# Layer 0's scores as one fp32r product of 128 rows, with its row term brought in by key quarters

## The reference

```python
B, H, W, C = 8, 32, 32, 96; NH, HD = 6, 16
# layer 0: group norm, attention with relative positions over 32x32 = 1024 tokens
attn  = einsum('bqd,bkd->bqk', q * HD**-0.5, k)
rel_h = einsum('bhwc,hkc->bhwk', r_q, Rh)          # by key row
rel_w = einsum('bhwc,wkc->bhwk', r_q, Rw)          # by key column
attn  = attn + rel_h[..., :, None] + rel_w[..., None, :]
x = x + (softmax(attn) @ v) @ proj_w + proj_b
# layer 1: layer norm, causal attention of 6 heads over the same 1024 tokens, then
# layer norm and 4 experts (96 -> 384 -> 96, GELU) of which the best 2 are mixed by a gate
```

## Time and profile before

| | |
|---|---|
| median of 3 runs | 2086.81 us (2080.82 to 2087.43) |
| profiled execution | 2086.0 us, span 2084.2 us |
| TensorE busy | 1821.2 us (87%), granted clock 0.94 |
| VectorE busy | 1248.4 us (60%) |
| ScalarE busy | 1119.9 us (54%) |
| GpSimd busy | 144.8 us (7%) |
| DMA | 111.02 MB, 27.8% of 16 engines on SyncE's queue |

### The profile page before, as it was taken

The page is one execution under the profiler, slowest core; times in us unless marked ns, Lnnn a source line. Parts: engine busy times, 40 slices in busy tenths (PEclk is TensorE's granted clock), DMA queues, the critical chain, the costliest instruction groups (busy, mean ns, idle before and its releaser), DMA issues.

```text
span 2084.2 us, 25918 instructions
## 1 busy us (share of the span) xinstructions
PE 1821.2 (87%) x9696; PEld 742.3 (36%) x9696; DVE 1248.4 (60%) x2508; ACT 1119.9 (54%) x1423; POOL 144.8 (7%) x69
## 2 busy tenths in 40 slices
PE   2698489998899988998899988999889988999858
PEld 1132233343334433343333433344333433334333
DVE  5671677546764577636775567636776466744631
ACT  2256345674456735675456744567355745555433
POOL 3000002000020000200020000200002000200000
PEclk7599589999999999999999999999999999999979
DMA  6416400344006320263003430164102630002100
GB/s 139 60 33 111 80 11 19 84 68 84 11 24 113 74 44 20 51 102 69 21 19 87 66 84 11 30 113 77 36 19 51 102 69 15 18 11 57 30 11 8
DMA packets 55701, 111.02 MB, mean 53 GB/s; under 512 B 17686, under 2 KB 18903, under 8 KB 54040
## 3 DMA queue, kind: packets, MB, share of 16 engines
q1 hardware_dynamic: 54040, 109.06, 27.8%
q10 hardware_dynamic: 1536, 0.30, 0.1%
HBM read 61.82 MB, written 34.60 MB: 46 GB/s over the span
## 4 chain that ended last, share of the span: by engine, by line
PE 67%; DVE 18%; ACT 6%; DMA 4%; issue 3%; SPq 1%; POOL 1%; ACTq 0%; DVEq 0%; POOLq 0%
PE psS L596 12%; PE psOM L647 9%; DVE mx L1289 8%; PE psT L625 8%; PE psT L626 7%; PE psT L765 5%; PE psOM L655 5%; PE psS L779 4%; PE psT L628 4%; DVE mrow L1391 3%; PE psT L546 3%; DVE qb L1418 2%; DVE x L1400 1%; PE psT L555 1%; DMA qr<-negb 1%
## 5 line engine op out<-in xcount | busy, mean ns | idle before, releaser
L1016 ACT ACTIVATE probs<-psT 128x1024 f32<-128x1024 f32 (+7 forms) x768 | 622.7, 837 | 511.0 <-PE psT L626 256.9
L1289 DVE TENSOR_REDUCE mx<-psS 128x1 f32<-128x512 f32 (+3 forms) x1152 | 705.1, 643 | 271.8 <-PE psS L596 207.7
L626 PE MATMUL psT<-qb,kb 97*128 97x512 f32 x768 | 414.5, 584 | 0.0
L596 PE MATMUL psS<-ka,qa 128*128 128x512 bf16 x768 | 302.6, 403 | 37.1 <-DVE mx L1289 16.4
L625 PE MATMUL psT<-qa,ka 128*128 128x512 bf16 x768 | 296.2, 386 | 11.7 <-DVE resid L1278 5.1
L647 PE MATMUL psOM<-probs,v 128*32 128x512 f32 x1536 | 207.1, 604 | 0.0
L628 PE MATMUL psT<-qr,kr 97*128 97x512 bf16 (+3 forms) x576 | 187.4, 354 | 4.2 <-DMA qr<-negb 3.2
L765 PE MATMUL psT<-xf,w1s 97*128 97x512 f32 x384 | 182.4, 608 | 2.0 <-DVE mrow L1391 1.8
L779 PE MATMUL psS<-probs,w2s 128*96 128x512 f32 x384 | 180.7, 596 | 0.8 <-ACT att L1081 0.8
L1418 DVE TENSOR_TENSOR qb<-psOM,qa 32x768 fp32r<-32x768 f32 x128 | 121.8, 952 | 96.6 <-ACT qa L1056 94.8
L596 PEld LDWEIGHTS psS<-ka,qa 128*128 128x128 bf16 x768 | 71.8, 98 | 302.4 <-DVE mx L1289 237.9
(11 more groups left out here) (148 smaller groups left out, 1705.3 us busy)
## 6 DMA issues: line engine op xcount, KB each, us to landing
scr<-split SPq DMA_DIRECT2D x32, 576.0 KB, 4.3
scr<-qb SPq DMA_DIRECT2D x16, 768.0 KB, 6.8
qr<-scr SPq DMA_DIRECT2D x48, 192.0 KB, 6.8
au<-ot SPq DMA_DIRECT2D x192, 32.0 KB, 2.0
lb<-ot SPq DMA_DIRECT2D x192, 32.0 KB, 2.0
qr<-scr SPq DMA_DIRECT2D x48, 128.0 KB, 4.3
kr<-scr SPq DMA_DIRECT2D x48, 128.0 KB, 7.0
qa<-scr SPq DMA_DIRECT2D x32, 128.0 KB, 3.9
```

The source lines that it names most:

```text
L596: last = mm(bank[:, 0:n], q[0:rows, h, t * P:(t + 1) * P], k[0:rows, h, kc * HALF:kc * HALF + n], start=True, stop=not diagonal)
L626: last = mm(o[:, a:b], kb[:, h, ks], qb[:, h, a:b], start=False, stop=True)
L1016: A(probs[:, n % 4, q0:T], psT[:, t_slot(ts, m), q0:T], ACT.Exp).then_inc(t_free, 1)
L1289: V.reduce_max(mx[layer][:, p % 2, (h % 2) * NT + t, kc:kc + 1], psS[:, s_bank(st, fill), 0:max_cols(layer, t, kc)], AX).then_inc(s_free, 1)
```

## The change

Layer 0's score becomes a single fp32r product of 128 rows, `ks[:, slot, head]` by `qs[:, slot, c, head]`. Its rows: 31 by key column, leading part (`W_HI`), one row with the maximum (31, `MAX_ROW`), 31 by key column, rest (`W_LO`), 8 by key row, leading part (`H_HI`), 8, rest (`H_LO`), and three 16-row products of fp32r parts of q and k (`S_PARTS`). Column 31's relative term is subtracted from the others in the table (`relt_w`), so that 31 rows do.

With 8 rows for the key row only a quarter of the keys (8 of 32 key rows, two key tiles) is covered at a time. `qs` holds two copies per pair (`c`), for quarters 0 and 1 at first; in key tiles 1 and 3 ScalarE sends two transfers each that put quarter 2 into copy 0 and quarter 3 into copy 1; TensorE waits for them ahead of key tiles 4 and 6. The maxima row goes into both copies, by two transfers. `qs` and `ks` hold two pairs (slot p % 2). Their rows come from memory: the relative terms are written to `rel` (which lies in `qs`), from there to `scr_rel` in memory (`relative`), and `load_pair` reads 17 transfers per pair: pairs 0 and 1 at the start of layer 1's attention (`first_pairs`), pair 2 once pair 0's last scores are made. The rows of `qa` for the maxima are cast by GpSimd from `rel` (`lead_rows`). The splitting of q and k for layer 0 is done by GpSimd alone (`operand_parts`, eleven operations); ScalarE only copies q and k out (`keep_qk`). `operands0` loads `qa` and `ka` in one go. The values of two heads share one block of ones (`vs`), in both layers.

```diff
+W_HI, MAX_ROW, W_LO, H_HI, H_LO, QK_ROWS = 0, HS - 1, HS, 2 * HS, 2 * HS + QROWS, 2 * HS + 2 * QROWS
+S_PARTS = ((0, 2), (0, 3), (1, 2))
...
+        qs = sb("qs", [P, 2, 2, 2, T], F32R)
+        ks = sb("ks", [P, 2, 2, T], F32R)
+        rel = qs[:, :, :, :, :].rearrange("p s c h t -> p (s c h) t")[:, 0:NH]
...
+        loads += [(il[a:a + WS - 1, :], w_hots) for a in (W_HI, W_LO)]
...
+        def quarter_rows(p, c, n):
+            heads, rows = slice(2 * p, 2 * p + 2), slice(n * QROWS, (n + 1) * QROWS)
+            return [(qs_raw[a:a + QROWS, p % 2, c], scr_rel[b:b + HS][rows, heads]) for a, b in ((H_HI, R_H_HI), (H_LO, R_H_LO))]
...
+            def load_pair(p):
+                heads, slot, done = slice(2 * p, 2 * p + 2), p % 2, pair_in[p % 2]
+                for c in range(2):
+                    sp.dma_start(qs_raw[W_HI:W_HI + WS - 1, slot, c], scr_rel[R_W_HI:R_W_HI + WS - 1, heads]).then_inc(done, 16)
+                    sp.dma_start(qs_raw[W_LO:W_LO + WS - 1, slot, c], scr_rel[R_W_LO:R_W_LO + WS - 1, heads]).then_inc(done, 16)
+                    for dst, src in quarter_rows(p, c, c):
+                        sp.dma_start(dst, src).then_inc(done, 16)
+                    for n, (q, _) in enumerate(S_PARTS):
+                        a = QK_ROWS + n * HD
+                        sp.dma_start(qs_raw[a:a + HD, slot, c], scr32_d[:, q, heads]).then_inc(done, 16)
+                for n, (_, k) in enumerate(S_PARTS):
+                    a = QK_ROWS + n * HD
+                    sp.dma_start(ks_raw[a:a + HD, slot], scr32_d[:, k, heads]).then_inc(done, 16)
+            def relative(it, st):
+                sp.wait_ge(rel_free, upto("rel_free", it, st, incs("rel_free", st, kind_of(it))))
+                sp.dma_start(scr_rel[:, 0:3], rel_raw[:, 0:3]).then_inc(spill_rel, 16)
+                sp.dma_start(scr_rel[:, 3:NH], rel_raw[:, 3:NH]).then_inc(spill_rel, 16)
+            def first_pairs(it, st):
+                sp.wait_ge(spill_rel, upto("spill_rel", it, st, 32))
+                sp.wait_ge(rel_lead_bf, upto("rel_lead_bf", it, st, NH))
+                load_pair(0)
+                load_pair(1)
...
             def attention1(it):
                 if next_layer0(it):
                     load_x(it + 2)
+                if next_lead(it):
+                    first_pairs(it - 1 if it else None, "mix")
                 for p in range(PAIRS):
                     gather(it, 1, p)
...
                             if layer == 0:
-                                mm(o[:, a:b], ka[:, h, ks], qa[:, h, a:b], start=True, stop=False)
-                                last = mm(o[:, a:b], kb[:, h, ks], qb[:, h, a:b], start=False, stop=True)
+                                last = mm(o[:, a:b], ks[:, p % 2, hh, keys], qs[:, p % 2, kt // 2 % 2, hh, a:b], start=True,
+                                          stop=True)
...
+                        pe.wait_ge(pair_in[p % 2], upto(("pair_a_in", "pair_b_in")[p % 2], it, st, PAIR_LOADS * (p // 2 + 1)))
...
+                        if layer == 0 and kt in (4, 6):
+                            c = kt // 2 % 2
+                            pe.wait_ge(turn_in[c], upto(("turn_a_in", "turn_b_in")[c], it, st, 32 * (p + 1)))
...
+                            if layer == 0 and hh == 1 and kt in (1, 3):
+                                for dst, src in quarter_rows(p, kt // 2, kt // 2 + 2):
+                                    act.dma_start(dst, src).then_inc(turn_in[kt // 2], 16)
...
+            def operand_parts(it, stage):
...
+            def lead_rows(it, stage):
...
+                for h in range(NH):
+                    nc.gpsimd.tensor_copy(qa[R_H_HI:P, h, :], rel_raw[R_H_HI:P, h, :]).then_inc(rel_lead_bf, 1)
```

More of the change, by code:

```diff
@@ L441, in spill_wide @@
[L441 to L450, removed]
+                sp.dma_start(scr32[:, 2], rest_of[1]).then_inc(spill_k, 16)
@@ L480, in attention0 @@
                 sp.dma_start(x0[:, :, :], x_tok[row]).then_inc(x0_in, 16)
+                st, n = att_t(0, 2 * NT - 1)
+                sp.wait_ge(t_full, upto("t_full", it, st, n + 1))
+                load_pair(2)
                 gather(it, 0, 0)
@@ L485, in attention0 @@
                 if next_layer0(it):
+                    sp.wait_ge(pair_in[0], upto("pair_a_in", it, "attn0", 2 * PAIR_LOADS))
                     spill_wide(it, "qkv0")
-                    operands0(slice(0, 4))
+                if next_layer0(it):
+                    operands0()
                 gather(it, 0, 2)
+                slots1(it)
                 if next_layer0(it):
-                    operands0(slice(4, NH))
-                slots1(it)
+                    relative(it, "mix")
             def store(it, row):
@@ L501, in _ @@
             spill_wide(None, "p_qkv0")
-            operands0(slice(0, 4))
-            operands0(slice(4, NH))
+            operands0()
+            relative(None, "p_rel")
+            first_pairs(None, "p_rel")
             attention0(None, 0)
@@ L654, in values @@
                             every = probs[:, (2 * kt + hh) % 4, :].rearrange("p (i c q) -> p c i q", c=NC, q=P)
-                            last = mm(psO[j:j + 2 * HD, first * P:HALF], v[:, kt, 2 * p + hh, :], every[:, c, first:],
+                            last = mm(psO[j:j + 2 * HD, first * P:HALF], v[:, kt, p, hh * HD:(hh + 2) * HD], every[:, c, first:],
                                       start=kt == 0, stop=kt == NT - NC + c)
@@ L978, in neg_max @@
                 act.wait_ge(m_free, upto("m_free", it, ms, n + 1))
-                row = (qb_raw, qr)[layer][C:C + 1, 2 * p:2 * p + 2, :]
-                act.dma_start(row.rearrange("o h (t q) -> o (h t) q", q=P),
-                              negm_raw[layer][:, p % 2, :]).then_inc(negmax_in, 16)
+                if layer == 0 and p == 0:
+                    act.wait_ge(spill_rel, upto("spill_rel", it, ms, 0))
+                rows = [qr[C:C + 1, 2 * p:2 * p + 2, :]] if layer else [qs_raw[MAX_ROW:MAX_ROW + 1, p % 2, c] for c in range(2)]
+                for row in rows:
+                    act.dma_start(row.rearrange("o h (t q) -> o (h t) q", q=P),
+                                  negm_raw[layer][:, p % 2, :]).then_inc(negmax_in, 16)
             def first_negated(it, st):
@@ L1107, in mix @@
                     elif what == "qk":
-                        levels_a(it, "mix", 1, n)
+                        levels_a(it, "mix", n)
                     elif what == "val":
@@ L1112, in mix @@
                         for s in range(2):
-                            levels_b(it, "mix", 1, s)
+                            levels_b(it, "mix", s)
             exp_table()
@@ L1158, in den @@
+            def lead_rows(it, stage):
+                pool.wait_ge(rel_lead, upto("rel_lead", it, stage, incs("rel_lead", stage, kind_of(it))))
+                pool.wait_ge(s_full, upto("s_full", it, "lead" if it is None else "mix", 0))
+                for h in range(NH):
+                    nc.gpsimd.tensor_copy(qa[R_H_HI:P, h, :], rel_raw[R_H_HI:P, h, :]).then_inc(rel_lead_bf, 1)
+                pool.wait_ge(rel_lead_bf, upto("rel_lead_bf", it, stage, NH))
             def den(it):
@@ L1215, in constants @@
                 ready(V.tensor_copy(mask_k[:, :], probs[:, 0, P:2 * P]))
-                for ones in (vs[0][:, :, :, HD:2 * HD], vs[1][:, :, :, HD:2 * HD]):
-                    ready(V.memset(ones, 1.0))
+                for v in vs:
+                    ready(V.memset(v[:, :, :, HD:2 * HD], 1.0))
                 ready(V.memset(mx[0][:, :, :, :], -BIG))
@@ L1463, in attention0 @@
             def attention0(it):
-                per = PER_PAIR[0]
-                if next_layer0(it):
-                    ahead = per + per * 5 // (5 * (NT - 2))
-                    maxima(it, "attn0", range(ahead))
-                    for s in range(2):
-                        residual(it, "qkv0", 0, s)
-                    maxima(it, "attn0", range(ahead, 2 * per))
-                else:
-                    maxima(it, "attn0", range(2 * per))
+                maxima(it, "attn0", range(2 * PER_PAIR[0]))
             group_stats(None, "p_gn")
```

233 lines of the change are left out of this document (141 added, 92 removed), and 3 rows, old and new, of the table INCS.

## The result

The changed kernel takes 2510.11 us (median of 4 runs, 2508.99 to 2517.42); the kernel before, on the same chip, 2087.12. The ratio is 1.204, 95% interval 1.2006 to 1.2075: 423 us slower. The forecast was 2325, in a range of 2130 to 2580.

What follows compares the result with a forecast made beforehand. TensorE was taken to lead, with VectorE or ScalarE soon next. Each round: 19 for gathers, 13 for pair 2's rows, 2 for clock, less 7 gained, +27; seven rounds +189, first batch +52, on 2086.0: 2325 us, range 2130 to 2580.

Steps and rivals of the forecast that it cites:

- The transfers: SyncE's pair loads: each 31-row transfer runs on one DMA engine, 0.34 us per 8 KB row, 46 us per pair.
- One product for two: Layer 0's attention: dropping the bf16 score products gives back about 7 us a round, if no transfer is late.
- (a): Layer 1's attention: gathers queued behind pairs 0 and 1's loads land at +98, wanted at +79: +19 us.
- (b): Layer 0's attention: pair 2's rows land 46 us after pair 1 begins, which lasts 33: TensorE waits 13 us.
- (c): ScalarE's maxima rows share the busy engine, 0 to 5 us each; delay before 588 swallowed by (a): nothing added.
- (d): Quarter refresh in pairs 1 and 2: about 9 and 4 us before its wait, against 1.8 us landing: hidden.
- (e): SyncE's spill, second gather and operand loads behind pair 2's rows: parts for the relative products hidden by 15 us.
- The first batch: Start of the kernel: pairs 0, 1 and 2 late by 31, 15 and 13 us, less 7 gained: +52.
- The sum: Whole kernel: +27 us a round seven times, +189, and +52 for the first batch: 2327, stated as 2325.
- the rival rate: Pair loads: one engine at the slower rate, 60 us per pair, round +70, 2670 us in all; chance 0.10.
- All transfers are spread: Rival on the pair loads: all engines share them, 2.4 MB per pair in 8 us, 2043 us; chance 0.13.
- spread, but refresh and maxima rows late: Rival: loads spread, but ScalarE's transfers meet them; 2 us lost per wait, +7 per round, 2135 us; chance 0.05.

Runs made afterwards that it cites:

- e1: The changed kernel with each 31-row transfer of load_pair cut into 16 and 15 rows, same bytes: 2174.51 us, ratio 1.0421.
- e4: The kernel before plus eight loads timed alone at its end: 31 rows of 8 KB 11.5 us, 32 rows 3.05, 16 rows 2.7, 15 rows 2.5.
- e10: The changed kernel, 31-row loads whole, with SyncE waiting after every seventh load of a pair until all have landed: 2652.21 us, ratio 1.2728.
- e3: The kernel before with layer 0's bf16 score product left out: 2013.88 us, ratio 0.9656.
- e7: e1 without ScalarE's quarter refreshes and TensorE's waits for them: 2142.37 us, ratio 1.0267.
- e8: e6 with the two 31-row loads of constants also cut into 16 and 15 rows: 2103.53 us, ratio 1.0087.
- e6: e1 with SyncE waiting after every seventh load of a pair until all have landed: 2103.93 us, ratio 1.0081.
- e9: e8 without waits after seven in layer 1's attention, pair 1's loads held there until its maxima row landed: 2097.58 us, ratio 1.0064.

## Why the prediction was right or wrong

*"The transfers": one engine for a 31-row transfer.* Right, and shown four ways: the share of 0.06, e1, e4 and e10. The size is the term of the sum that was too small: "One 8 KB row is 0.34 us", "46 us per pair". In the first batch the rows of three pairs are loaded one behind the other, and TensorE waits for each. The first load is issued at 86.36, and TensorE begins the pairs at:

```profile
139.95 0.77 PE L687 MATMUL psT<-qs,ks 128*128 128x512 f32 x1 [34.53 <-issue]
...
192.76 0.77 PE L687 MATMUL psT<-qs,ks 128*128 128x512 f32 x1 [22.20 <-issue]
...
245.09 2.04 PE L687 MATMUL psT<-qs,ks 128*128 128x512 f32 x4 [18.65 <-issue]
```

A pair therefore took 53.6, 52.8 and 52.3 us, by an estimate 0.38 to 0.39 us for each of the 137 rows (four times 31, and one of each other load) that I had on the engine. Why they are dearer than 0.34 was not tried.

*"One product for two": "a round gives back about 7 us".* The size was near: e3 gave 9 a batch. The working was off by one term: I took 0.69 us per reduce as VectorE's floor and let the gap shrink. The gap stayed, and VectorE took a reduce every 0.60 us. Pair 0's pace after is 3.08 + 0.61 = 3.69 us for five, near the predicted 3.73; that they meet is luck.

*(a) The gathers, +19.* Right in kind and mis-sized: ScalarE gets the gathers at 748.38, +112 and not +98, which is 33 us later in the round than in the kernel before. Two pairs at 53 us instead of 46 make 13 of the 14 us that are missing. ScalarE's idle time at L1109 is 14.2 us and not 33 only because ScalarE itself came some 18 us late.

*(b) Pair 2's rows, TensorE waits 13 us.* It waited 13.8, but partly by luck. The rows took 56.5 us from the first issue (763.98) to TensorE's start, not 2 + 46. Against that, they were asked for 7.8 us before pair 1 began, not 2, and pair 1 without the wait lasted 35.0 us, not 33: 56.5 - 7.8 - 35.0 = 13.8.

*(c) The maxima rows: "what that delays before 588 is swallowed by (a), so nothing is added".* This holds. The rows took 4.4 to 4.7 us at the median (8.6 at most), TensorE waited 3.4, 6.0 and 6.3 us for them, and layer 1's attention grew by 17.8 us. But the chain of that round runs along SyncE's issues from 636.63 to 738.21 and then through the last gather to 748.38, past all of these rows: without them ScalarE would have waited longer at L1109. e10 shows the same, with a shorter attention and a longer round. The row before pair 1 took 7.8 us, more than the "0 to 5"; it lies beside pair 2's loads, which were asked for before it landed. The rows cost time where the loads are spread, as in e1.

*(d) The refresh: "hidden".* Nearly right for the changed kernel, though the landing of 1.8 us that I gave it was wrong: it landed after 10.0 us in pair 1 and 5.7 in pair 2, since I had not asked what SyncE would have in flight just then. TensorE stood 1.1 and 0.6 us for it, the first of them ahead of the longer wait for pair 2's rows; in all rounds together it was 22.3 us. With all engines spread the refresh cost 32 us in the whole (e7).

*(e) Operands behind pair 2's rows, hidden.* Right in the changed kernel: the mix kept its 80.5 us.

*The first batch, +52.* TensorE reached pair 0 at 139.95 instead of 100.49: +39 against 31, and 7.6 of the 8 are again the price of a pair's rows. Then it waited 22.2 and 18.7 us for the next two pairs, where I had 15 and 13. With the first round in it, the first store was +127 late where 52 + 27 = 79 were forecast. The two 31-row constants I had as 5 us each of an engine; in the chain one alone was 10.7 us, and with both cut the first store came 11 us sooner (e8 against e6).

*The sum.* Forecast +27 a round; measured +46 in the middle one. Cut where the chain shows the limit, that is +33 until the gathers are there (forecast 19), +16 from there to the start of pair 2, and -2 in pair 2 (forecast -2.9). The missing 19 us are, to the size that these figures allow, the price of a pair's rows: 14 us ahead of the gathers, and 8.5 us in the 56.5 us of pair 2's rows, less what the other terms gave back. The mechanism was the forecast one; 46 us a pair was too little, and the 60 us of the rival rate too much.

*The rivals.* "All transfers are spread" at 2043 and "spread, but refresh and maxima rows late" at 2135 were both tried in effect by e1: 2174, near the second of them. I had it as an alternative to one engine only; it is what came to light once one engine was no longer the limit. The 2043 rested on 8 us for a pair's 2.4 MB at 292 GB/s; in e1 a pair takes 17 us.

## What to carry to other kernels

Read the row count of each new transfer before its bytes: 29 and 31 rows ran on one engine here, 30 and 32 did not. Cutting 31 rows into 16 and 15 costs one issue of 0.4 us and, by the times of e4, saves some 8 us (an estimate). Then ask of each small transfer on a wait path what the other queue has in flight at that moment: its landing in a quiet trace (1.7 us) is a lower bound, and up to 14 us were seen. Read a late landing as a loss only where the chain that decides passes through it: 17.8 us of delay in layer 1's attention were free while the gathers came later still, and such rows cost time once the loads were fast (e1). No version here beat the kernel before: the best, e9, is 0.6% slower, although one product for two by itself is worth 3.4% (e3).

## What the runs showed that was not expected

- SyncE is held at issue while one engine is behind: up to 18.6 us for two issues. The gathers queued behind were issued only after it.
- 16 engines at a share of 1.05 moved 152 GB/s in the pair loads of e1, where other stretches showed 292 at 0.75. So a busy share of 1 does not tell the rate; why this traffic is slower was not tried.
- ScalarE's own queue is no way past SyncE's. The Trainium skill (DMA: Bandwidth & Descriptors, "Queues, rings and completion order") says that an engine alternates between queues packet by packet. The 11.9 and 14.0 us of e1 are how long ScalarE's transfers took here all the same; what such a turn lasts no run shows.
- Reduces of VectorE overlap: one of 512 columns lasts 0.68 to 0.69 us, and the next begins after 0.60 once TensorE issues one score product for two (e3, e1 and the changed kernel show 3.08 us for five). The time of one is no floor for the step.
